# Second attention of a two-layer language model: softmax by TensorE in PSUM after the turn, instead of ScalarE and VectorE before it

## The chip, the cores and the metric

The kernel runs on one NeuronCore of a Trainium2 chip. The metric is the device time of the whole program in microseconds. Before the change it is 5177.2 us, the median of 3 runs (5175.48 to 5177.86).

## What is computed

Two batches of 1024 tokens of width 1024 pass through a token map and two layers; each layer is an attention and a mixture of low-rank experts, each behind a layer norm and added to its input. The change lies in the second attention. It has 32 query heads and 8 key and value heads of 32 columns, and it keeps, in each query's row, only the 128 largest scores:

```python
draft = jnp.einsum('bhqd,bhkd->bhqk', qr, kr)
draft = draft + jnp.where(causal_future, neg, jnp.asarray(0.0, dtype))
_, draft_indices = jax.lax.top_k(draft, num_remain)
mask = jnp.full((B, H, Sq, Sq), neg, dtype)
mask = mask.at[b_idx, h_idx, s_idx, draft_indices].set(0.0)
mask = jnp.where(causal_future[None, None, :, :], neg, mask)
scores = jnp.einsum('bhqd,bhkd->bhqk', qr, kr) / np.sqrt(HD).astype(np.float32) + mask
attn = jax.nn.softmax(scores, axis=-1)
out = jnp.einsum('bhqk,bhkd->bhqd', attn, v)
```

Here `num_remain` is 128 and the rows have up to 1024 keys.

## The kernel before

The program is a sequence of blocks: token map, projection, first attention, mixture, projection, second attention (`kept_attention`, L807), last mixture. Each block writes its engines' instruction streams by hand, and semaphores order them; nothing is scheduled by a compiler.

`kept_attention` works on 32 pairs of heads (m = 0, 1). The queries of a head are 8 tiles i of 128 rows. Tile i has (i + 1) x 128 keys, so a pair's lower triangle is 2 x 36 blocks of 128 x 128, SEG = 4608 columns a head. The work is a pipeline over slots s (L870): in slot s

- the scores of pair s + 1 are computed by TensorE (`scores`, L926) and fetched from PSUM by VectorE with the row's maximum (`fetch`, L1262);
- pair s is searched: in five passes p ScalarE counts how many scores of a row lie under a threshold (`count`, L1014, a Sign with a running sum, L1030), VectorE counts the two narrowest tiles itself (`count_short`, L1087), and `narrow` (L1134) makes the next threshold from the counts. L1127 (`start`) and L1166 (the end of `narrow`) increment the semaphore `t_ready` that ScalarE waits for, and ScalarE's `signs_done` is what `narrow` waits for ahead of L1140;
- pair s - 1 is chosen and kept: `rank_some` (L1180) and `choose` (L1188) find the limit exactly, and `keep` (L1252) multiplies the exponentials by (score >= limit), with the row sum (L1257);
- pair s - 2 goes to the values stage: TensorE turns the blocks (`turn`, L942), ScalarE copies them to `probT` (`evac`, L993), TensorE multiplies by V (`values`, L958), and VectorE normalises (`normalise`, L1270).

The exponentials of pair s are made by ScalarE behind its counts of passes 2, 3 and 4 (`exps`, L1036), with the negated maximum as bias. The row sums are inverted in pass 4 (`invert`, L1278), spread over 512 columns, turned by TensorE (`turn_inverse`, L950) and copied to `invT` (L999). Scores x have two buffers, the exponentials two more in `arena`, `ps_t` has three banks and `ps_o` one.

Which part of VectorE's work comes in which pass is written out by hand (`part`, L1311): the ranks in passes 0 and 1, `choose` at the end of 1; keeps of 7, 5 and 2 tiles in passes 2, 3, 4; fetches of 4, 8 and 4 tiles there; `normalise` at the end of pass 2. ScalarE's 24 evacuations stand between and behind its counts of passes 0 and 1 (`evacs`, L1010), the last four of each pass behind all its counts. TensorE's stream in a slot is the inverse's turn, then for every two chunks two turns and the value products of the two chunks before, and at last the 16 score tiles, two of which fit ahead of VectorE's fetches. SP's queue loads queries and keys a group (two pairs) ahead, stores the outputs of a slot, and loads the next values when they are stored (L894).

Slots run from -1 to 33. Those from 4 to 29 are a hardware loop whose body is two slots (L878).

The values stage in TensorE's stream:

```python
if n >= 2:
    pe.wait_ge(probT_ready, (s - 2) * TURNED + (n - 1))
for c in range(0, w, P):
    at = ps_seg(m, i) + a + c
    mm = nc.tensor.transpose(ps_t[:, (n + 1) % 3, c:c + P], prob[:, par, at:at + P], ident[:, :])
mm.then_inc(turn_done, 1)
```

## Time and profile before

| what | value |
|---|---|
| median of 3 runs | 5177.2 us |
| profiled execution: its own time | 5178.5 us |
| profiled execution: span, first to last instruction | 5176.7 us |
| PE busy, share of the span | 3755.9 us, 73% |
| VectorE (DVE) busy | 3509.0 us, 68% |
| ScalarE (ACT) busy | 3166.3 us, 61% |
| mean granted TensorE clock | 0.831 of full speed |

The page also draws the span in 40 slices of about 129 us. The second attention takes slices 18 to 37, from about 2250 to 4855 us: there VectorE shows 8 tenths and ScalarE 9 in nearly every slice, PE about 5, with a granted clock of 6 to 7 tenths.

A line of a group reads: line, engine, operation, output <- inputs by the program's names, their shapes, count, then busy us and mean ns of one, then the engine's idle time just before these instructions and what ended it. "issue" is time in which the engine waited for nothing that the profile shows. Busy time alone does not tell what sets the end of a stage; the order in time and the waits do.

### The profile page before, as it was taken

The page shows a single profiled execution, that of the slowest core. Times are in us where ns is not written, and L with a number is a line of the kernel's source. Part 1 is how long each engine was busy: PE and PEld are TensorE (multiplying, and loading weights), DVE is VectorE, ACT ScalarE, POOL GpSimd, SP SyncE. Part 2 cuts the span into 40 slices and gives each one's busy share as a digit, 9 for nine tenths or more (in the row PEclk, how much of TensorE's full clock was granted, in tenths as well). Part 3 has the DMA queues.
Part 4 walks back from the last instruction along what each step waited for, and adds up shares of the span by engine and source line. Part 5 has one row for each costly group of instructions (what it writes and reads, how often), then busy time and mean ns, then how long its engine had stood idle before and what let it go on. Part 6 is the DMA issues. An engine that isn't in the chain of part 4 may idle for free. (4 is left out here: it accounts for less than half of the span.)

```text
span 5176.7 us, 79684 instructions
## 1 busy us (share of the span) xinstructions
PE 3755.9 (73%) x23338; PEld 2210.1 (43%) x23480; DVE 3509.0 (68%) x10383; ACT 3166.3 (61%) x7058; POOL 288.7 (6%) x213
## 2 busy tenths in 40 slices
PE   6998999998999999934555355555555555554699
PEld 2444766666444444412333233333333333332454
DVE  3654777776333356548888888888888888887444
ACT  1123777776000011259999599999999999999200
POOL 2332000000000023300000000000000000000000
PEclk9999999999999999966766566767766667766899
DMA  3325223232211112310111011110011110110222
GB/s 139 74 64 162 71 61 79 53 78 82 68 49 49 44 46 69 85 41 1 26 27 26 1 26 26 25 25 12 18 26 26 23 26 4 26 26 6 78 86 77
DMA packets 276875, 249.81 MB, mean 48 GB/s; under 512 B 170048, under 2 KB 209232, under 8 KB 276432
## 3 DMA queue, kind: packets, MB, share of 16 engines
q1 hardware_dynamic: 275888, 245.13, 18.0%
q14 instruction: 324, 2.65, 0.2%
q8 instruction: 119, 1.95, 0.2%
q0 software_dynamic: 544, 0.07, 0.0%
HBM read 167.56 MB, written 77.59 MB: 47 GB/s over the span
## 5 line engine op out<-in xcount | busy, mean ns | idle before, releaser
L1030 ACT ACTIVATE a_sign<-a_x,a_state 128x384 fp8e4<-128x384 f32 (+5 forms) x1536 | 1343.0, 876 | 126.3 <-DVE a_state L1166 87.9
L936 PE MATMUL a_ps_s<-k,q 128*128 128x512 bf16 (+3 forms) x1474 | 500.7, 486 | 692.0 <-DVE a_x L1267 661.7
L947 PE MATMUL a_ps_t<-ident,arena 128*128 128x128 f32 x2304 | 484.6, 355 | 194.3 <-ACT a_invT L999 130.6
L936 PEld LDWEIGHTS a_ps_s<-k,q 128*128 128x128 bf16 x1536 | 168.6, 131 | 916.3 <-DVE a_x L1267 749.8
L965 PE MATMUL a_ps_o<-a_probT,vals 128*32 128x128 f32 x4608 | 404.9, 325 | 185.1 <-ACT a_probT L995 184.7
L947 PEld LDWEIGHTS a_ps_t<-ident,arena 128*128 128x128 f32 x2304 | 338.6, 180 | 333.4 <-ACT a_invT L999 143.4
L721 ACT ACTIVATE a_prob<-a_x_neg,a_shift 128x640 f32<-128x640 f32 (+7 forms) x512 | 397.1, 776 | 80.4 <-DVE a_x_neg L764 61.9
L1267 DVE TENSOR_SCALAR_CACHE_REDUCE a_x<-a_ps_s 128x128 f32<-128x128 f32 (+7 forms) x512 | 383.7, 754 | 85.2 <-PE a_ps_s L939 59.9
L995 ACT COPY a_probT<-a_ps_t 128x512 f32<-128x512 f32 (+3 forms) x768 | 345.9, 475 | 111.1 <-PE a_ps_t L947 110.5
L764 DVE TENSOR_SCALAR_CACHE_REDUCE a_x_neg<-a_ps_s 128x640 f32<-128x640 f32 (+7 forms) x512 | 378.7, 751 | 38.8 <-PE a_ps_s L645 25.6
L1177 DVE MAX8 a_nine<-a_below 128x8 f32<-128x256 f32 (+6 forms) x448 | 371.0, 828 | 32.9
L965 PEld LDWEIGHTS a_ps_o<-a_probT,vals 128*32 128x32 f32 x4608 | 266.6, 128 | 293.9 <-ACT a_probT L995 267.9
L660 PE MATMUL a_ps_t<-ident,a_prob 128*128 128x128 f32 x2304 | 363.7, 281 | 33.4 <-ACT a_prob L721 19.6
L1257 DVE SCALAR_TENSOR_TENSOR arena<-a_x,a_limit,arena 128x1024 f32<-128x1024 f32 (+6 forms) x449 | 379.2, 878 | 5.1 <-issue 4.5
L1174 DVE SCALAR_TENSOR_TENSOR a_below<-a_last,a_x 128x256 f32<-128x256 fp8e4 (+6 forms) x448 | 362.3, 809 | 7.5 <-ACT a_last L1030 7.4
L642 PE MATMUL a_ps_s<-k,q 128*128 128x512 bf16 (+3 forms) x1456 | 320.1, 326 | 26.8 <-DVE a_x_neg L764 12.3
L347 PE MATMUL p_ps_qkv<-wqkv,p_hT 128*128 128x512 f32 x768 | 337.8, 597 | 1.7 <-ACT p_hT L385 1.2
L347 PE MATMUL p_ps_qkv<-arena,p_hT 128*128 128x512 f32 x768 | 337.8, 597 | 1.6 <-ACT p_hT L385 1.2
L1030 ACT ACTIVATE a_last<-a_x,a_state 128x384 fp8e4<-128x384 f32 (+5 forms) x384 | 333.1, 868 | 5.2
L774 DVE COPY a_probT<-a_ps_t 128x384 f32<-128x384 f32 (+3 forms) x384 | 221.6, 577 | 166.8 <-PE a_ps_t L660 165.3
L1042 ACT ACTIVATE arena<-a_x,a_shift 128x256 f32<-128x256 f32 (+6 forms) x448 | 334.0, 813 | 0.0
L385 ACT COPY p_hT<-p_ps_h 128x512 f32<-128x512 f32 x64 | 34.4, 589 | 440.9 <-PE p_ps_h L334 440.9
(216 smaller groups left out, 5947.7 us busy)
## 6 DMA issues: line engine op xcount, KB each, us to landing
q<-qk SPq DMA_DIRECT2D x256, 256.0 KB, 4.9
qk<-p_qkT SPq DMA_DIRECT2D x32, 960.0 KB, 6.2
h_rows<-h SPq DMA_DIRECT2D x32, 512.0 KB, 6.8
k<-qk SPq DMA_DIRECT2D x256, 64.0 KB, 5.2
m_o<-o SPq DMA_DIRECT2D x32, 512.0 KB, 5.5
m_h<-h SPq DMA_DIRECT2D x32, 512.0 KB, 5.3
h<-tok_h SPq DMA_DIRECT2D x16, 512.0 KB, 4.0
arena<-in_wo SPq DMA_DIRECT2D x16, 512.0 KB, 11.3
```

The lines of the kernel that those rows point to most:

```text
L347: m = nc.tensor.matmul(ps_qkv[:, n * BANK:(n + 1) * BANK], hT[:, par, k * P:(k + 1) * P], w[:, k, n * BANK:(n + 1) * BANK], start=(k == 0) ...
L660: mm = nc.tensor.transpose(ps_t[:, n % 2, c * P:(c + 1) * P], prob[:, s % 2, (a + c) * P:(a + c + 1) * P], ident[:, :])
L721: nc.scalar.activation(prob[:, s % 2, 0:w], x_neg[:, s % 4, 0:w], ACT.Exp, scale=-1.0, bias=shift[:, s % 4:s % 4 + 1], accum_out=total[:, ...
L764: nc.vector.tensor_scalar(x_neg[:, c, 0:w], ps_s[:, s % 2, 0:w], -1.0, None, ALU.mult, ALU.min, accum_out=shift[:, c:c + 1]).then_inc(shif ...
L936: nc.tensor.matmul(ps_s[:, n % 2, a:a + w], q[:, y, head, i * P:(i + 1) * P], k[:, y, a:a + w], start=(y == 0), stop=False, skip_group_che ...
L947: mm = nc.tensor.transpose(ps_t[:, (n + 1) % 3, c:c + P], prob[:, par, at:at + P], ident[:, :])
L965: mm = nc.tensor.matmul(ps_o[strip:strip + DH, c:c + P], v[:, at * DH:(at + 1) * DH], probT[:, (n + m) % 4, b * P:(b + 1) * P], start=(at ...
L1030: ins = nc.scalar.activation(to, x[:, par, at:at + w], ACT.Sign, scale=-1.0, saturate=False, bias=state[:, par, 0, n:n + 1], accum_out=sta ...
L1174: lambda: nc.vector.scalar_tensor_tensor(out=below[:, r, 0:w], in0=last[:, at:at + w], scalar=2 * WIDE if n in SHORT else WIDE, in1=x[:, y ...
L1177: lambda: nc.vector.max(nine[:, n, 1:9], below[:, r, 0:w]),
L1257: return nc.vector.scalar_tensor_tensor(out=prob[:, y, at:at + w], in0=x[:, y, at:at + w], scalar=limit[:, r:r + 1], in1=prob[:, y, at:at ...
L1267: nc.vector.tensor_scalar(x[:, y, at:at + w], ps_s[:, n % 2, 0:w], 1.0, None, ALU.mult, ALU.max, accum_out=top[:, y, n:n + 1]).then_inc(x_ ...
```

## The change

- `keep` becomes `mark` (VectorE): it writes a bf16 mask, 0 or -1e18, from the scores and the limit, with no multiplication and no row sum.
- The exponentials of x on ScalarE in passes 2 to 4 are removed. TensorE turns the scores themselves, and adds to the turned block in PSUM the negated maximum of each query (as three bf16 parts that add up to it, turned once a slot, and spread over the keys by a matmul with a matrix of ones in three rows) and the turned mask (70 matmuls of 128 columns a slot; the first tile of a head has none). ScalarE's evacuation is the exponential.
- V has 32 columns of ones beside its 32 columns, so each head's products have their row sums in 32 rows of PSUM below the outputs. `ps_o` has two banks for that, `ps_t` two instead of three.
- `normalise` takes the reciprocal of all of `ps_o`, 128 x 1024, and multiplies each head's 32 rows by the sums' inverses. `invert`, `turn_inverse` and the copy to `invT` are gone; the maximum's turn and its copy of 48 rows stand in their place.
- Scores have three buffers, two of them in `arena`, since a score lives until its turn. So the slots repeat only after 6, and the loop's body is six slots: 4 to 27 are in the loop.
- VectorE waits in pass 2 for the last turn ahead of its marks, since there is one mask buffer; it no longer waits for the exponentials. PE's turn waits one evacuation sooner than before, having a bank less.

```diff
         c_at, t_at = g * P + (2 * y + m) * DH, b * T
-        sp.dma_start(o_dram[ds(c_at, DH), ds(t_at, T)].rearrange("d (h c) -> h d c", h=2),
-                     o[2 * m * DH:(2 * m + 2) * DH, :]).then_inc(done, 16)
+        sp.dma_start(o_dram[ds(c_at, DH), ds(t_at, T)], o[2 * m * DH:(2 * m + 1) * DH, :]).then_inc(done, 16)
...
         probT = sb("probT", [P, 4, BANK])
-        o = sb("o", [P, BANK])
+        o, inv = sb("o", [P, T]), sb("inv", [P, T])
         sign, last = sb("sign", [P, SEG + P], FP8), sb("last", [P, 2 * SEG], FP8)
         below = sb("below", [P, 2, T])
-        top, shift = sb("top", [P, 2, 2 * TT]), sb("shift", [P, 2, 2 * TT])
-        total, inv = sb("total", [P, 2, 2 * TT]), sb("inv", [P, 2 * TT])
-        inv_wide, invT = sb("inv_wide", [P, BANK]), sb("invT", [P, BANK])
+        top, rest = sb("top", [P, 2 * TT]), sb("rest", [P, 2 * TT])
+        top_b = sb("top_b", [P, 2, 2 * TT], BF16)
+        top_parts, topT = sb("top_parts", [P, 3, P]), sb("topT", [SPLITS * 2 * TT, P], BF16)
+        row_of, rows = sb("row_of", [SPLITS * 2 * TT, 2 * TT, P], BF16), sb("rows", [SPLITS * 2 * TT, 2 * TT])
...
+        ps_s, ps_t, ps_o = ps("ps_s", [P, 2, 2 * BANK]), ps("ps_t", [P, 2, BANK]), ps("ps_o", [P, 2 * BANK])
...
         def over_slots(eng, slot):
 
             for s in range(-1, FIRST_LOOP):
-                slot(s, s % 2, stages(s))
+                slot(s, s % BODY, stages(s))
             with eng.Fori(0, LOOPS) as r:
-                for c in (0, 1):
-                    slot(r * 2 + (FIRST_LOOP + c), c, ALL)
-            for s in range(FIRST_LOOP + 2 * LOOPS, PAIRS + 2):
-                slot(s, s % 2, stages(s))
+                for c in range(FIRST_LOOP, FIRST_LOOP + BODY):
+                    slot(r * BODY + c, c % BODY, ALL)
+            for s in range(FIRST_LOOP + BODY * LOOPS, PAIRS + 2):
+                slot(s, s % BODY, stages(s))
...
                     def turn(n, m, i, a, w):
-                        if n >= 2:
-                            pe.wait_ge(probT_ready, (s - 2) * TURNED + (n - 1))
+
+                        to = ps_t[:, (n + 1) % 2, 0:w]
+                        pe.wait_ge(probT_ready, (s - 2) * TURNED + max(n, 1))
                         for c in range(0, w, P):
                             at = ps_seg(m, i) + a + c
-                            mm = nc.tensor.transpose(ps_t[:, (n + 1) % 3, c:c + P], prob[:, par, at:at + P], ident[:, :])
+                            nc.tensor.matmul(to[:, c:c + P], xs[old][:, at:at + P], ident[:, :], start=(c == 0), stop=False,
+                                             is_transpose=True, skip_group_check=True)
+                        mm = nc.tensor.matmul(to.rearrange("p (b c) -> p b c", c=P), row_of[:, m * TT + i, :],
+                                              topT[:, :].unsqueeze(1).to_broadcast([SPLITS * 2 * TT, w // P, P]),
+                                              start=False, stop=(i == 0), skip_group_check=True)
+                        for c in range(0, w if i else 0, P):
+                            at = ps_seg(m, i) + a + c
+                            mm = nc.tensor.matmul(to[:, c:c + P], mask[:, at:at + P], ident_b[:, :], start=False,
+                                                  stop=True, skip_group_check=True)
                         mm.then_inc(turn_done, 1)
 
-                    def turn_inverse():
-                        pe.wait_ge(inv_ready, s - 1)
+                    def turn_top():
+                        pe.wait_ge(top_ready, s - 1)
                         if not (isinstance(s, int) and s == 2):
                             pe.wait_ge(probT_ready, (s - 2) * TURNED)
-                        for c in range(0, BANK, P):
-                            mm = nc.tensor.transpose(ps_t[:, 0, c:c + P], inv_wide[:, c:c + P], ident[:, :])
-                        mm.then_inc(turn_done, 1)
+                        nc.tensor.transpose(ps_t[:, 0, 0:P], top_parts[:, old, :], ident[:, :]).then_inc(turn_done, 1)
...
+                                half, at = 2 * m * DH, a // P + b
+                                mm = nc.tensor.matmul(ps_o[half:half + 2 * DH, i * P:(i + 1) * P], v[:, at, :],
                                                       probT[:, (n + m) % 4, b * P:(b + 1) * P], start=(at == 0),
-                                                      stop=(at == i), tile_position=(0, strip))
+                                                      stop=(at == i), tile_position=(0, half))
...
+                        pe.wait_ge(mask_ready, (s - 2) * NS + NS)
                         if not (isinstance(s, int) and s == 2):
                             pe.wait_ge(o_ready, s - 2)
-                        turn_inverse()
+                        turn_top()
...
+
                     def evac(n, m, i, a, w):
                         act.wait_ge(turn_done, (s - 2) * TURNED + (n + 2))
-                        nc.scalar.copy(probT[:, n % 4, 0:w], ps_t[:, (n + 1) % 3, 0:w]).then_inc(probT_ready, 1)
-
-                    def inverse_evac():
+                        nc.scalar.activation(probT[:, n % 4, 0:w], ps_t[:, (n + 1) % 2, 0:w], ACT.Exp).then_inc(probT_ready, 1)
+
+                    def top_evac():
                         act.wait_ge(turn_done, (s - 2) * TURNED + 1)
-                        nc.scalar.copy(invT[:, :], ps_t[:, 0, :]).then_inc(probT_ready, 1)
+                        nc.scalar.copy(topT[:, :], ps_t[0:SPLITS * 2 * TT, 0, 0:P]).then_inc(probT_ready, 1)
...
-                    def exps(n, y):
-
-                        m, i = TILES[n]
-                        at, w = ps_seg(m, i), (i + 1) * P
-                        if i:
-                            ins = nc.scalar.activation(prob[:, y, at:at + w], x[:, y, at:at + w], ACT.Exp,
-                                                       bias=shift[:, y, n:n + 1])
-                        else:
-                            ins = nc.scalar.activation(prob[:, y, at:at + w], x[:, y, at:at + w], ACT.Exp,
-                                                       bias=shift[:, y, n:n + 1], accum_out=total[:, y, n:n + 1])
-                        ins.then_inc(exp_done, 1)
-
-
-                    EXPS = {2: range(0, 6), 3: range(6, 11), 4: range(11, 2 * TT)}
                     for p in range(PASSES):
                         if st["search"]:
                             count(p)
                         else:
                             for n in range(NS):
                                 evacs(p * NS + n)
-                        if st["search"] and p in EXPS:
-                            if p == 2 and st["value"]:
-                                act.wait_ge(turn_done, (s - 2) * TURNED + TURNED)
-                            for n in EXPS[p]:
-                                exps(n, par)
 
...
                 nc.vector.memset(two[:, :], 2.0)
+                nc.vector.memset(top_parts[:, :, :], 0.0)
+                nc.vector.memset(v[:, :, DH:2 * DH], 1.0)
+                of = [ident[0:SPLITS * 2 * TT, c * 2 * TT:(c + 1) * 2 * TT] for c in range(SPLITS)]
+                nc.vector.tensor_tensor(rows[:, :], of[0], of[1], ALU.add)
+                dve.drain()
+                nc.vector.tensor_tensor(rows[:, :], rows[:, :], of[2], ALU.add)
+                dve.drain()
+                nc.vector.tensor_copy(row_of[:, :, :], rows[:, :].unsqueeze(2).to_broadcast([SPLITS * 2 * TT, 2 * TT, P]))
                 quantile, per_sign, aim = (table[:, k_, :] for k_ in range(3))
...
-                        nc.vector.tensor_scalar(shift[:, z, :], top[:, z, :], -1.0, None, ALU.mult)
+                        hi, mid, lo = (top_parts[:, (turn_of + 1) % 3, c * 2 * TT:(c + 1) * 2 * TT] for c in range(SPLITS))
+                        nc.vector.tensor_scalar(top_b[:, 0, :], top[:, :], -1.0, None, ALU.mult)
                         dve.drain()
                         nc.vector.tensor_scalar(var_h[:, :], var[:, :], -0.5, None, ALU.mult)
-                        dve.drain()
+                        nc.vector.scalar_tensor_tensor(out=rest[:, :], in0=top[:, :], scalar=-1.0, in1=top_b[:, 0, :],
+                                                       op0=ALU.mult, op1=ALU.subtract)
+                        nc.vector.tensor_copy(hi, top_b[:, 0, :])
+                        dve.drain()
+                        nc.vector.tensor_copy(top_b[:, 1, :], rest[:, :])
+                        dve.drain()
+                        nc.vector.tensor_copy(mid, top_b[:, 1, :])
+                        nc.vector.tensor_tensor(lo, rest[:, :], top_b[:, 1, :], ALU.subtract).then_inc(top_ready, 1)
...
-                    def keep(r):
...
+                    def mark(r):
 
                         m, i = RANKED[r]
-                        n = TILES.index((m, i))
                         at, w = ps_seg(m, i), (i + 1) * P
-                        return nc.vector.scalar_tensor_tensor(out=prob[:, y, at:at + w], in0=x[:, y, at:at + w],
-                                                              scalar=limit[:, r:r + 1], in1=prob[:, y, at:at + w],
-                                                              op0=ALU.is_ge, op1=ALU.mult,
-                                                              accum_out=total[:, y, n:n + 1])
+                        return nc.vector.tensor_scalar(mask[:, at:at + w], old_x[:, at:at + w], limit[:, r:r + 1], MASKED,
+                                                       ALU.is_lt, ALU.mult)
...
-                        nc.vector.tensor_scalar(x[:, y, at:at + w], ps_s[:, n % 2, 0:w], 1.0, None, ALU.mult, ALU.max,
-                                                accum_out=top[:, y, n:n + 1]).then_inc(x_ready, 1)
+                        nc.vector.tensor_scalar(new_x[:, at:at + w], ps_s[:, n % 2, 0:w], 1.0, None, ALU.mult, ALU.max,
+                                                accum_out=top[:, n:n + 1]).then_inc(x_ready, 1)
 
                     def normalise():
 
                         dve.wait_ge(pv_done, (s - 2) * (NC // 2) + NC // 2)
-                        dve.wait_ge(probT_ready, (s - 2) * TURNED + 1)
                         if not (isinstance(s, int) and s == 2):
                             dve.wait_ge(o_out, (s - 2) * 32)
-                        nc.vector.tensor_tensor(o[:, :], ps_o[:, :], invT[:, :], ALU.mult).then_inc(o_ready, 1)
-
-                    def invert():
-
-                        dve.drain()
-                        nc.vector.reciprocal(inv[:, :], total[:, y, :])
-                        dve.drain()
-                        nc.vector.tensor_copy(inv_wide[:, :].rearrange("p (j q c) -> p j q c", j=4, q=4),
-                                              inv[:, :].rearrange("p (q j) -> p j q", j=4).unsqueeze(3).to_broadcast(
-                                                  [P, 4, 4, DH])).then_inc(inv_ready, 1)
+                        nc.vector.reciprocal(inv[:, :], ps_o[:, :])
+                        dve.drain()
+                        for m in range(2):
+                            half = 2 * m * DH
+                            ins = nc.vector.tensor_tensor(o[half:half + DH, :], ps_o[half:half + DH, :],
+                                                          inv[half + DH:half + 2 * DH, :], ALU.mult)
+                        ins.then_inc(o_ready, 1)
 
...
-                                dve.wait_ge(exp_done, (s - 1) * (2 * TT) + 2 * TT)
+                        if p == 2 and st["value"]:
+                            dve.wait_ge(turn_done, (s - 2) * TURNED + TURNED)
...
-                                keep(r).then_inc(prob_ready, 1)
+                                mark(r).then_inc(mask_ready, 1)
...
-                        if p == 4 and st["keep"]:
-                            invert()
+                        if p == 4:
+                            dve.drain()
                         if p == 4 and st["score"]:
-                            dve.drain()
...
-        vals1 = sb(ctx, "vals1", [P, TT * DH])
+        vals1 = sb(ctx, "vals1", [P, TT, 2 * DH])
```

## Rows read from the trace of the kernel before

**Rows 1.** Windows: length, busy us (xcount) of PE, PEld, DVE, ACT, POOL, granted clock.

```profile
2390.00:4835.00 2445.00, 1340.05 (x8630) 821.51 (x8687) 2072.01 (x6573) 2222.78 (x4935) 0.00 (x0) 0.69 0.09 21
```

**Rows 2.** VectorE's timeline, one slot: start us, us, engine, line, operation, [idle before].

```profile
4171.10 0.17 DVE L1127 SCALAR_TENSOR_TENSOR a_state<-a_mean,a_tmp 128x14 f32<-128x14 f32 x1
...
4250.13 0.17 DVE L1127 SCALAR_TENSOR_TENSOR a_state<-a_mean,a_tmp 128x14 f32<-128x14 f32 x1
...
4265.78 0.18 DVE L1166 COPY_PREDICATED a_state<-a_open,a_new 128x14 f32<-128x14 int32 x1
...
4282.90 0.17 DVE L1140 TENSOR_TENSOR a_state<-a_state,search 128x14 f32<-128x14 f32 x1 [1.67 <-ACT a_sign L1030]
...
4284.81 0.18 DVE L1166 COPY_PREDICATED a_state<-a_open,a_new 128x14 f32<-128x14 int32 x1
...
4299.13 0.18 DVE L1166 COPY_PREDICATED a_state<-a_open,a_new 128x14 f32<-128x14 int32 x1
...
4313.19 0.18 DVE L1166 COPY_PREDICATED a_state<-a_open,a_new 128x14 f32<-128x14 int32 x1
...
4327.50 0.17 DVE L1127 SCALAR_TENSOR_TENSOR a_state<-a_mean,a_tmp 128x14 f32<-128x14 f32 x1
...
4330.90 0.48 DVE L1095 SCALAR_TENSOR_TENSOR a_sign<-a_x,a_state,a_two 128x256 fp8e4<-128x256 f32 x1 [2.81 <-issue]
```

**Rows 3.** Groups by line, the second attention, ScalarE.

```profile
L1042 ACT ACTIVATE arena<-a_x,a_shift 128x896 f32<-128x896 f32 x415 | 310.0, 814 | 0.0
...
L995 ACT COPY a_probT<-a_ps_t 128x128 f32<-128x128 f32 (+1 forms) x744 | 335.2, 475 | 108.2 <-PE a_ps_t L947 107.6
```

**Rows 4.** Groups by shape, before 2500 us, ScalarE.

```profile
L237 ACT ACTIVATE tok_h<-tok_ps_h 128x1024 f32<-128x1024 f32 x16 | 16.0, 1025 | 18.5 <-PE tok_ps_h L223 15.8 <-DMA h<-tok_h 2.7
```

**Rows 5.** Groups by shape, the second attention, VectorE.

```profile
L1257 DVE SCALAR_TENSOR_TENSOR arena<-a_x,a_limit,arena 128x1024 f32<-128x1024 f32 x62 | 79.0, 1275 | 0.1
...
L1257 DVE SCALAR_TENSOR_TENSOR arena<-a_x,a_limit,arena 128x256 f32<-128x256 f32 x60 | 28.9, 482 | 4.8 <-issue 4.5
...
L1276 DVE TENSOR_TENSOR a_o<-a_ps_o,a_invT 128x512 f32<-128x512 f32 x31 | 21.3, 686 | 22.4 <-PE a_ps_o L965 21.9 <-issue 0.5
...
L1159 DVE RECIPROCAL a_rs<-a_span 128x14 f32<-128x14 f32 x88 | 21.2, 241 | 6.4
...
L1100 DVE TENSOR_SCALAR a_last<-a_x,a_state 128x256 fp8e4<-128x256 f32 x60 | 18.5, 350 | 4.3
...
L1281 DVE RECIPROCAL a_inv<-a_total 128x16 f32<-128x16 f32 x31 | 7.8, 253 | 7.1 <-issue 5.7
```

**Rows 6.** Groups by shape, before 2400 us, VectorE.

```profile
L106 DVE TENSOR_SCALAR arena<-h_rows,p_mv,p_rstd 128x1024 f32<-128x1024 f32 x32 | 26.0, 813 | 2.5
...
L1638 DVE TENSOR_TENSOR m_y<-m_ps_y,m_h 128x1024 f32<-128x1024 f32 x16 | 19.6, 1225 | 155.9 <-PE m_ps_y L1501 155.9
...
L779 DVE RECIPROCAL a_inv<-a_total 128x8 f32<-128x8 f32 x64 | 12.3, 192 | 0.0
```

**Rows 7.** TensorE's timeline, two slots: turns, bias and score matmuls, values.

```profile
3563.38 1.97 PE L947 MATMUL a_ps_t<-ident,arena 128*128 128x128 f32 x8
...
3583.05 0.22 PE L939 MATMUL a_ps_s<-a_bias_b,a_ident_b 128*128 128x128 bf16 x1
...
3583.11 0.38 PE L936 MATMUL a_ps_s<-k,q 128*128 128x256 bf16 x2
...
3608.15 0.97 PE L936 MATMUL a_ps_s<-k,q 128*128 128x512 bf16 x4
...
3608.95 0.22 PE L939 MATMUL a_ps_s<-a_bias_b,a_ident_b 128*128 128x128 bf16 x1
...
4851.34 1.09 PE L947 MATMUL a_ps_t<-ident,arena 128*128 128x128 f32 x8
...
4852.36 1.94 PE L965 MATMUL a_ps_o<-a_probT,vals 128*32 128x128 f32 x32
```

**Rows 8.** VectorE's timeline, last normalisation of the second attention.

```profile
4854.35 0.69 DVE L1276 TENSOR_TENSOR a_o<-a_ps_o,a_invT 128x512 f32<-128x512 f32 x1 [21.89 <-PE a_ps_o L965]
```

66 lines of the change are left out of this document (33 added, 33 removed).

## The prediction

> **What bounds the kernel now.** I read the busy time by stage first. Over the 2445 us of the second attention VectorE is busy 2072 us and ScalarE 2223 us [rows 1]. ScalarE has the larger sum, so it looks like the bound, but both are close together, and neither sum tells who waits for whom. So next comes VectorE's timeline, at the instructions that hand a new threshold to ScalarE (L1127 once a slot, L1166 four times) [rows 2]. From one to the next the passes last 15.65, 19.03, 14.32, 14.06 and 14.31 us: a slot of 77.4 us. The slot before took 79.0 (4171.10 to 4250.13), the mean is 78.2. In this slot VectorE waits for ScalarE's counts only in pass 1, 1.67 us ahead of L1140. Otherwise it goes from one of its own instructions to the next. So VectorE sets passes 0, 2, 3 and 4, and ScalarE, with the values stage of TensorE that it evacuates, sets the end of pass 1. Without that wait passes 0 and 1 would take 34.7 - 1.7 = 33.0 us. In every second slot VectorE also stands 2.81 us for nothing that the profile shows, at the first instruction behind the loop's return [rows 2].
>
> This decides what the parts are worth: what leaves ScalarE in passes 2 to 4 is nearly free of profit, what VectorE gains or loses there counts in full.
>
> **ScalarE.** The exponentials of x go, 16 a slot at 814 ns, some 13 us [rows 3]. All lie in passes 2 to 4, beside VectorE. The only part on the path is the tail by which pass 0's counts start late, about 1 us. The 24 evacuations become exponentials. From PSUM with no bias the nearest row is the tanh, 1025 ns for 1024 columns [rows 4], against 475 ns for 384 on average of the copies [rows 3]: 0.86 ns a column between them, the columns' own rate, so I take no extra (at most 24 x 0.1 us).
>
> **VectorE, marks.** 14 keeps, from 482 ns at 256 columns to 1275 at 1024 [rows 5], so 880 at the mean of 640, become one-source mask writes with no sum. The nearest rows of that kind are 350 ns at 256 columns [rows 5] and 813 at 1024 [rows 6], so 0.6 ns a column instead of 1.03, and 565 to 580 on average. That saves 0.3 us each, 4.2 us a slot: 2.1 in pass 2 (7 marks), 1.1 in pass 3 (5 mostly narrow), 0.95 in pass 4 (2 wide). If the bf16 result forces one column at a time, it is 350 + 768 x 1.03 = 1140 at 1024, and the saving only 1.6 us a slot.
>
> **VectorE, normalise.** Today it is one multiply of 512 columns, 686 ns [rows 5]. It becomes a reciprocal of 1024 columns out of PSUM, then two multiplies of 1024 columns, one behind the other, at 1225 ns each [rows 6] less overlap, 2.4 us together. The reciprocal is the term that matters. The trace has it at 8 columns, 192 ns [rows 6], at 14, 241 ns, and at 16, 253 ns [rows 5]. A copy or an add doesn't get dearer by 61 ns over 8 columns; a reciprocal does: (253 - 192) / 8 = 7.6 ns a column. 1024 columns then take 0.13 + 1024 x 7.6 ns = **7.9 us**. Bounds: from 14 to 16 columns 6 ns, 6.3 us; from 8 to 14 columns 8.2 ns, 8.5 us. The least that I admit is a plain one-column rate, 1.2 us, a rival below. The sum is 7.9 + 0.1 + 2.4 - 0.7 = +9.7 us, all of it in pass 2 between the fetches and the narrowing, where nobody else does VectorE's work. Queued behind it are L1140 and so ScalarE's next counts.
> The Trainium skill ("VectorE: DVE Perf Modes", First, the fixed hardware budget) says that the reciprocal is an iterative divide with a repeat count of 8; with that page's 0.96 GHz I estimate 8.3 ns a column, 8.5 us, and the total would be some 20 us above mine. It speaks against this change, and the rows above agree.
>
> **VectorE, the rest.** invert() goes: its reciprocal of 253 ns, a copy of 512 columns and two drains, 0.8 us in pass 4. The bf16 splits of the maximum add five operations of 14 to 16 columns, 0.17 us each as L1140 in rows 2, with two drains between them: 0.85 us. They cancel.
> New waits: in pass 2 the marks wait for the last turn. By rows 2 pass 2 begins when that stage has just ended, and VectorE gets there over 2 us later, so it costs nothing; it is charged below if the stage grows. PE's first turn waits for the evacuated maximum, ScalarE's first work in a slot, as the inverse does today. SP's queue has the same steps: the stores stand 27 us ahead of what needs them, and the values' load with 128-byte rows has that cover too.
>
> **TensorE.** Three of the four turns of the inverse go, one is left for the maximum. Added per slot: 70 mask matmuls of 128 columns in bf16, the same as the causal bias, which is followed after 0.06 us at the full clock [rows 7], 4.2 us; and 24 row matmuls, 9216 columns in all, by the score matmuls, four of 512 in 0.80 us [rows 7], 3.6 us. So +7.8 us at 2.4 GHz on 18.0 (72 turns at 0.128, 144 value matmuls at 0.061, [rows 7]), and about twice both at 1.2 GHz, where eight turns last 1.97 us instead of 1.09. The granted clock averages 0.69 [rows 1], since PE idles between evacuations; more work in the stage gives fewer idle gaps. 26 to 30 us of work fit into 34.7 us by length, but PE has two score banks, not three, and ScalarE takes the four last chunks of a pass in one go. I take 36 us for passes 0 and 1, between 33.0 (PE and ScalarE fully hidden) and 34.7 + 7.8 = 42.5 (all added work on the path).
>
> **The sum.** Pass 2: 14.3 - 2.1 + 9.7 = 21.9. Pass 3: 14.1 - 1.1 = 13.0, and 13.1 with ScalarE's counts so close under it. Pass 4: 14.3 - 0.95 + 0.05 = 13.4. With 36.0 that is 84.4, and 0.4 for the loop's return, one slot in six: 84.8 us, **+6.6 a slot**, for 30 slots +198. Slot 32 has no counting: -4.2 + 9.7 - 0.8 = +4.7. In slot 33 the values stage stands alone, VectorE waits 21.89 us for it [rows 8]: +7.8 + 9.7 - 0.7 = +16.8. Set-up and first slots: about -0.5. In all +219 us. The profiled execution took 5178.5 us (span 5176.7), 1.3 above the median of the runs, so I forecast 5396 against the median of 5177.2.
>
> **Rivals.** (a) *The reciprocal streams.* The slope of three tiny shapes might not hold over 1024 columns: then it takes 1.2 us, 6.7 less in 32 slots, 5182, and with passes 0 and 1 at their lower end of 33.0 another 90 less, 5092, faster. The point from which it decides is 7.9 - 219 / 32 = 1.1 us for the reciprocal, about 1 ns a column. Against it: three rows on one line of 6 to 8 ns a column. 0.07, of which 0.05 faster.
> (b) *TensorE becomes the bound of passes 0 and 1.* With them at 42.5 us it is 6.5 x 30 = 195 more, 5591. For it: pass 1 already ends on ScalarE and PE, a bank less, and value matmuls with 64 columns of weights instead of 32. If the two halves no longer run side by side, the stage is 9 us longer still. Against it: one slot in two ends by VectorE alone, and idle PE time is there to fill. 0.13. The Trainium skill ("TensorEngine Tiling (Array Packing)", When to Use Tiling) gives 64-column weights two tiles where 32-column ones have four; since the two heads alternate between halves before and after, my sum needs only two.
> (c) *The marks run at one column a cycle.* 2.6 us less saved in 31 slots, +80, 5476. Against it: the fp8 write of 256 columns takes 350 ns where the form with two sources takes 482. 0.1.
> (d) *ScalarE was the bound after all*, and 13 us of exponentials leave the path: then passes 2 to 4 would fall by more than VectorE allows; rows 2 exclude that, and it would come out as (a) at best.
> My forecast has 0.7.
>
> **Numbers.** Own range: reciprocal 6.3 to 8.5 (-51, +20), passes 0 and 1 a few us either way. Down to 5310 and up to 5510 it takes in (c) and half of (b). A measurement of this kernel can tell 0.2%, 10 us, from no change. Faster 0.05 and same 0.02 come from (a); slower 0.93 is the rest.
>
> **What would show it.** The reciprocal's row at 1024 columns, 6.3 to 8.5 us, 32 times; pass 2 at 22 us, passes 3 and 4 at 13 to 13.5; ScalarE busy well under 80% with idle time ended by L1166; mark rows near 570 ns; the mask matmuls 0.06 us apart. Wrong, if the reciprocal's row is under 2 us, or if the time between L1127 and the second L1166 leaves 33 to 40 us.

## The result and the profile after

The changed kernel takes 5380.95 us (median of 4 runs, 5373.36 to 5382.62), the kernel before 5176.34 on the same chip (4 runs). The ratio is 1.0392, interval 1.0374 to 1.041: **slower by 205 us**, where 219 had been forecast. The profiled execution took 5373.36 us (span 5371.5).

First the page of the changed kernel, busy time by engine and the groups that the change touches:

```profile
PE 4044.9 (75%) x26250; PEld 2322.1 (43%) x26392; DVE 3622.6 (67%) x10099; ACT 2837.9 (53%) x6482; POOL 289.1 (5%) x213
...
L1008 ACT ACTIVATE a_probT<-a_ps_t 128x512 f32<-128x512 f32 (+3 forms) x768 | 365.4, 483 | 289.1 <-PE a_ps_t L959 262.2
...
L954 PE MATMUL a_ps_t<-a_topT,a_row_of 48*128 48x512 bf16 (+3 forms) x768 | 289.1, 376 | 0.0
...
L959 PE MATMUL a_ps_t<-a_ident_b,a_mask 128*128 128x128 bf16 x2240 | 275.7, 242 | 0.0
```

ScalarE's evacuations now hold the exponential and last 483 ns on average, where the copies of [rows 3] lasted 475. What is new stands behind the bar: ScalarE waits 262 us for the mask matmul that ends a chunk (108 for the turn in [rows 3]). In the values stage it's TensorE that comes late, more than twice as much as before.

Next VectorE's groups by shape over the second attention:

```profile
L1283 DVE RECIPROCAL a_inv<-a_ps_o 128x1024 f32<-128x1024 f32 x32 | 209.7, 6554 | 39.9 <-PE a_ps_o L976 39.4 <-issue 0.5
...
L1287 DVE TENSOR_TENSOR a_o<-a_ps_o,a_inv 32x1024 f32<-32x1024 f32 x64 | 77.9, 1217 | 2.8
...
L1267 DVE TENSOR_SCALAR a_mask<-arena,a_limit 128x1024 bf16<-128x1024 f32 x45 | 33.4, 741 | 0.1
...
L1267 DVE TENSOR_SCALAR a_mask<-arena,a_limit 128x640 bf16<-128x640 f32 x44 | 23.8, 542 | 0.0
...
L1151 DVE TENSOR_TENSOR a_state<-a_state,search 128x14 f32<-128x14 f32 x128 | 22.3, 174 | 211.9 <-ACT a_sign L1043 206.7 <-issue 4.1
...
L1267 DVE TENSOR_SCALAR a_mask<-arena,a_limit 128x256 bf16<-128x256 f32 x44 | 15.5, 351 | 11.1 <-PE a_ps_t L959 8.0 <-issue 2.7
```

One reciprocal of 6.55 us a slot is the largest group: 210 us, more than the whole difference. The row of L1151 is the instruction that waits for ScalarE's counts; it now waits 207 us in all for ScalarE, against 81 before (L1140). Slot by slot in the timeline, the wait at the end of pass 1 is over 1.7 us in each of slots 4 to 28, and at the end of pass 0 some 3.2 us in 22 of these 25. Before, both stood at 0.7 and 1.7 us, and in one slot of two alone: not in those in which VectorE stands 2.8 us at the loop's return, since it is late itself there.

VectorE's timeline shows pass 2 of one slot, from one handed threshold (L1177) to the next (columns as in [rows 2]):

```profile
3486.52 0.17 DVE L1151 TENSOR_TENSOR a_state<-a_state,search 128x14 f32<-128x14 f32 x1 [1.78 <-ACT a_sign L1043]
...
3488.42 0.18 DVE L1177 COPY_PREDICATED a_state<-a_open,a_new 128x14 f32<-128x14 int32 x1
...
3491.08 3.33 DVE L1267 TENSOR_SCALAR a_mask<-arena,a_limit 128x256 bf16<-128x256 f32 x7 [0.16 <-issue]
...
3496.80 6.55 DVE L1283 RECIPROCAL a_inv<-a_ps_o 128x1024 f32<-128x1024 f32 x1
3503.43 2.45 DVE L1287 TENSOR_TENSOR a_o<-a_ps_o,a_inv 32x1024 f32<-32x1024 f32 x2
3506.05 0.17 DVE L1151 TENSOR_TENSOR a_state<-a_state,search 128x14 f32<-128x14 f32 x1 [0.17 <-issue]
...
3507.95 0.18 DVE L1177 COPY_PREDICATED a_state<-a_open,a_new 128x14 f32<-128x14 int32 x1
```

L1151 at 3506.05 waits for nobody: VectorE sets the end of this pass, and 9.0 of its 19.5 us are the normalisation. The windows of the five passes of this slot and of the whole stage, columns as in [rows 1]:

```profile
3451.00:3469.20 18.20, 16.84 (x108) 9.74 (x108) 14.02 (x40) 14.73 (x35) 0.00 (x0) 0.69 0.00 1
3469.20:3488.50 19.30, 17.30 (x162) 10.95 (x161) 15.51 (x49) 15.45 (x36) 0.00 (x0) 1.00 0.01 1
3488.50:3508.00 19.50, 7.41 (x66) 4.51 (x65) 17.65 (x40) 11.68 (x26) 0.00 (x0) 0.70 0.01 2
3508.00:3521.00 13.00, 8.18 (x32) 3.54 (x32) 11.16 (x41) 10.60 (x24) 0.00 (x0) 0.66 0.00 1
3521.00:3533.90 12.90, 3.11 (x10) 1.28 (x11) 11.77 (x41) 10.60 (x24) 0.00 (x0) 0.74 0.41 95
2387.80:4950.00 2562.20, 1579.49 (x11128) 904.59 (x11186) 2130.70 (x6178) 1889.07 (x4343) 0.00 (x0) 0.74 0.09 19
```

In passes 0 and 1 TensorE is busy 34.1 of 37.5 us (the first busy time behind the length; the second is its weight loads), VectorE 29.5, ScalarE 30.2. Over the stage ScalarE fell to 74% of the time, from 91% in [rows 1], and that bought next to nothing.

Taken from such timelines, the passes have these lengths in us, as means over slots 2 to 30 without slot 8, whose exact selection lasts some 56 us in both kernels. All later pass lengths are made in this way. The forecast's 84.8 holds 0.4 for the loop's return.

| | pass 0 | 1 | 2 | 3 | 4 | 0 + 1 | slot |
|---|---|---|---|---|---|---|---|
| before | 16.8 | 18.3 | 14.5 | 14.0 | 14.5 | 35.1 | 78.1 |
| after | 18.1 | 19.7 | 20.0 | 13.0 | 13.0 | 37.8 | 83.8 |
| forecast | | | 21.9 | 13.1 | 13.4 | 36.0 | 84.8 |

### The profile page after: what moved, and what is told of

It is laid out like the page before. It is cut to its first block and busy times, and to the rows that moved or that the text cites. A ratio compares the mean times of both kernels' runs of the same rounds, so it can differ in the third digit from the quotient of the medians.

```text
span 5371.5 us, 84339 instructions
## 1 busy us (share of the span) xinstructions
PE 4044.9 (75%) x26250; PEld 2322.1 (43%) x26392; DVE 3622.6 (67%) x10099; ACT 2837.9 (53%) x6482; POOL 289.1 (5%) x213
## 3 DMA queue, kind: packets, MB, share of 16 engines
q1 hardware_dynamic: 289072, 245.14, 17.5%
## 5 line engine op out<-in xcount | busy, mean ns | idle before, releaser
L1043 ACT ACTIVATE a_sign<-arena,a_state 128x384 fp8e4<-128x384 f32 (+5 forms) x1056 | 917.6, 871 | 206.3 <-DVE a_state L1177 167.2
L1008 ACT ACTIVATE a_probT<-a_ps_t 128x512 f32<-128x512 f32 (+3 forms) x768 | 365.4, 483 | 289.1 <-PE a_ps_t L959 262.2
L1043 ACT ACTIVATE a_sign<-a_third,a_state 128x384 fp8e4<-128x384 f32 (+2 forms) x480 | 417.3, 871 | 139.2 <-DVE a_state L1177 136.3
L952 PE MATMUL a_ps_t<-ident,arena 128*128 128x128 f32 x1584 | 335.5, 328 | 201.6 <-ACT a_topT L1012 154.7
L976 PE MATMUL a_ps_o<-a_probT,vals 128*64 128x128 f32 x4608 | 362.4, 299 | 0.0
L1275 DVE TENSOR_SCALAR_CACHE_REDUCE arena<-a_ps_s 128x128 f32<-128x128 f32 (+3 forms) x352 | 262.9, 755 | 46.1 <-PE a_ps_s L943 21.6
L659 PEld LDWEIGHTS a_ps_t<-ident,a_prob 128*128 128x128 f32 x2304 | 247.9, 141 | 101.7 <-issue 36.1
L954 PE MATMUL a_ps_t<-a_topT,a_row_of 48*128 48x512 bf16 (+3 forms) x768 | 289.1, 376 | 0.0
L976 PEld LDWEIGHTS a_ps_o<-a_probT,vals 128*64 128x64 f32 x4608 | 265.7, 147 | 42.8 <-issue 15.9
L959 PE MATMUL a_ps_t<-a_ident_b,a_mask 128*128 128x128 bf16 x2240 | 275.7, 242 | 0.0
```

The lines of the kernel that those rows point to most:

```text
L659: mm = nc.tensor.transpose(ps_t[:, n % 2, c * P:(c + 1) * P], prob[:, s % 2, (a + c) * P:(a + c + 1) * P], ident[:, :])
L952: nc.tensor.matmul(to[:, c:c + P], xs[old][:, at:at + P], ident[:, :], start=(c == 0), stop=False, is_transpose=True, skip_group_check=True)
L954: mm = nc.tensor.matmul(to.rearrange("p (b c) -> p b c", c=P), row_of[:, m * TT + i, :], topT[:, :].unsqueeze(1).to_broadcast([SPLITS * 2 ...
L976: mm = nc.tensor.matmul(ps_o[half:half + 2 * DH, i * P:(i + 1) * P], v[:, at, :], probT[:, (n + m) % 4, b * P:(b + 1) * P], start=(at == 0 ...
L1008: nc.scalar.activation(probT[:, n % 4, 0:w], ps_t[:, (n + 1) % 2, 0:w], ACT.Exp).then_inc(probT_ready, 1)
L1043: ins = nc.scalar.activation(to, xs[mine][:, at:at + w], ACT.Sign, scale=-1.0, saturate=False, bias=state[:, par, 0, n:n + 1], accum_out=s ...
```

## The experiments

Ratios are to the kernel before, run on the same chips: 5172.44 us beside the first experiments, 5173.18 beside the next, 5174.61 beside the last three. The theory after the first profile: the reciprocal costs what the kernel lost, and the matmuls added to the values stage cost a second, smaller part that the lighter marks pay for.

### The reciprocal cut to 16 columns

```diff
-                        nc.vector.reciprocal(inv[:, :], ps_o[:, :])
+                        nc.vector.reciprocal(inv[:, 0:16], ps_o[:, 0:16])
```

> The changed kernel with the reciprocal cut to 16 of its 1024 columns (the other columns are multiplied by 1, so all but the first 16 queries of each head are not normalised). All else stays. Theory A, the forecast's: the reciprocal, 6554 ns in the profile of the changed kernel, stands alone on the path of pass 2. Pass 2 falls from 19.6 us by 6.3 to 13.3, just above the 12.8 us that ScalarE's counts and the narrowing need, and the kernel by 6.3 x 32 = 200 us, to about 5180. Theory B, TensorE's longer values stage is what costs and the reciprocal only fills time that VectorE would wait anyway: less than 60 us, so above 5320.

Measured: 5207.92 us, ratio 1.0065 (1.0049 to 1.0082), so 173 us of the 205 go with it (on another chip; by the ratios it's 169). Each of 32 reciprocals became 6.30 us shorter (6554 - 253 ns), 202 us in all, so some 29 us didn't come back. The pass lengths tell where they went: pass 2 is 14.6 us instead of the 13.7 (20.0 - 6.3) that VectorE's own work would need. VectorE's timeline of the pass and ScalarE's beside it:

```profile
3748.86 0.18 DVE L1178 COPY_PREDICATED a_state<-a_open,a_new 128x14 f32<-128x14 int32 x1
...
3761.49 0.17 DVE L1152 TENSOR_TENSOR a_state<-a_state,search 128x14 f32<-128x14 f32 x1 [1.49 <-ACT a_sign L1043]
```

```profile
3749.23 0.60 ACT L1008 ACTIVATE a_probT<-a_ps_t 128x512 f32<-128x512 f32 x1 [1.34 <-PE a_ps_t L959]
3750.32 0.60 ACT L1008 ACTIVATE a_probT<-a_ps_t 128x512 f32<-128x512 f32 x1 [0.49 <-PE a_ps_t L959]
3750.81 0.61 ACT L1043 ACTIVATE a_sign<-arena,a_state 128x384 fp8e4<-128x384 f32 x1
```

The threshold is ready at 3748.86, but ScalarE's queue still holds the last two evacuations, for which it waits on TensorE. Its counts begin 1.95 us late, and VectorE waits 1.49 us for them at the end. VectorE waits there for the counts in nearly every slot, and the pass ends at 14.5 to 14.6 us in nearly all. **There is a second floor under pass 2, 14.5 us, set by the tail of the values stage.** In the changed kernel it lies hidden under the reciprocal. That the tail sets it is read from the timeline; no run shortens the tail alone.

### The reciprocal added to the kernel before

```diff
                         nc.vector.tensor_tensor(o[:, :], ps_o[:, :], invT[:, :], ALU.mult).then_inc(o_ready, 1)
+                        nc.vector.reciprocal(below[:, 1, :], below[:, 0, :])
```

> The kernel before with one reciprocal of 1024 columns, from SBUF to SBUF, ahead of its normalising multiply, whose result nobody uses; in that kernel the two buffers are free there. Theory A: it takes 6.5 us as in the changed kernel and pass 2 of the kernel before is VectorE's, so each of 32 slots is 6.5 us longer: 208 us, about 5385. Theory B: ScalarE's exponentials in passes 2 to 4 leave room, and less than 60 us show. If a reciprocal from SBUF is quicker than one from PSUM, its row tells.

Measured: 5374.73 us, ratio 1.039 (1.0373 to 1.0407), +202 us, and its group reads:

```profile
L1276 DVE RECIPROCAL a_below<-a_below 128x1024 f32<-128x1024 f32 x32 | 209.6, 6548 | 21.9 <-PE a_ps_o L965 21.4 <-issue 0.5
```

Pass 2 goes from 14.5 to 20.7 us; the others stay within 0.2. One instruction a slot, with nothing else of the change, makes the kernel before as slow as the changed one. It reads SBUF, the changed kernel PSUM, and both take 6.55 us.

### What a reciprocal costs by size

```diff
+                nc.vector.memset(third[:, :], 1.5)
+                dve.drain()
+                for size in (8, 16, 32, 64, 128, 256, 512, 1024):
+                    nc.vector.reciprocal(inv[:, 0:size], third[:, 0:size])
+                    dve.drain()
```

> The changed kernel with eight more reciprocals ahead of its first slot, SBUF to SBUF, every input 1.5, of 8, 16, 32, 64, 128, 256, 512 and 1024 columns. The forecast's line, 0.13 us and 7.6 ns a column, gives 7.9 us at 1024, the changed kernel shows 6554 ns from PSUM. Theory D: the rate is 6.2 to 6.4 ns a column at every width, as from 14 to 16 columns, and the row of 8 columns has a smaller fixed part: about 0.33 us at 32, 1.7 at 256, 3.3 at 512, 6.5 at 1024. Theory E: small shapes cost 7.6 ns a column, and the rate falls with the width: 0.37 us at 32, and the slope between 32 and 64 is still over 7 ns. If the rate hangs on the values or on PSUM, 1024 columns of 1.5 from SBUF differ from 6554 ns.

One run, with these lines added to the set-up of the changed kernel. The groups by shape:

```profile
L1073 DVE RECIPROCAL a_inv<-a_third 128x1024 f32<-128x1024 f32 x1 | 6.6, 6554 | 0.1
...
L1073 DVE RECIPROCAL a_inv<-a_third 128x128 f32<-128x128 f32 x1 | 1.0, 953 | 0.1
...
L1073 DVE RECIPROCAL a_inv<-a_third 128x32 f32<-128x32 f32 x1 | 0.4, 354 | 0.1
...
L1073 DVE RECIPROCAL a_inv<-a_third 128x8 f32<-128x8 f32 x1 | 0.2, 203 | 0.1
```

From 8 to 1024 columns the cost is 0.153 us and 6.25 ns a column: (6554 - 203) / 1016. It is the column count that costs, neither the values nor where they lie. This run took 5404.15 us, and nothing is concluded from its time. The 8-column row of [rows 6] shows 192 ns, where this line gives 203. Those 11 ns, spread over 8 columns, made my slope 7.6.
The Trainium skill ("VectorE: DVE Perf Modes", First, the fixed hardware budget) has an iterative divide with a repeat count of 8; with the page's 0.96 GHz I had estimated 8.3 ns a column. The runs show 6.25, which by that clock I estimate at 6 cycles a column. That a reciprocal costs far more than one cycle a column, the run confirms; that the repeat count is the number of cycles, it does not.

### The changed kernel without the row and mask matmuls

```diff
                                 mm = nc.tensor.matmul(to[:, c:c + P], xs[old][:, at:at + P], ident[:, :], start=(c == 0),
-                                             stop=False, is_transpose=True, skip_group_check=True)
-                        mm = nc.tensor.matmul(to.rearrange("p (b c) -> p b c", c=P), row_of[:, m * TT + i, :], ...)
-                        for c in range(0, w if i else 0, P):
-                            mm = nc.tensor.matmul(to[:, c:c + P], mask[:, at:at + P], ident_b[:, :], ...)
+                                             stop=(c + P == w), is_transpose=True, skip_group_check=True)
```

> The changed kernel without the 24 row matmuls and 70 mask matmuls of a slot: TensorE turns the scores and ScalarE takes their exponential with no maximum taken off and nothing masked. Theory A: passes 0 and 1 are held by the length of TensorE's work, busy 34.1 of 37.5 us; without some 8 us of it they fall to what VectorE alone needs, 33.0 to 34.5 us, 3 to 4.5 us in 31 slots, so 95 to 140 us less, 5240 to 5285. Theory C, the stage is held by the alternation of TensorE and ScalarE over two banks and not by the length of the work: passes 0 and 1 stay above 36.5 us and the kernel falls by less than 35 us.

Measured: 5241.75 us, ratio 1.0138 (1.0121 to 1.0155), 139 us less than the changed kernel. Passes 0 and 1 are 34.1 us together instead of 37.8, the others keep their lengths within 0.2. That makes 3.7 us a slot, 110 in 30 slots, in the stretch where I had charged 0.9 over before. VectorE's waits for the counts fall back to what they are in the kernel before (0.6 and 1.0 us on average in passes 0 and 1, against 0.5 and 1.0). So the lost bank and the 64 columns of weights, which this run keeps, don't lengthen these passes. The rest of the 139 lies behind the last counting slot, where the stage stands alone. The windows of slot 33's values stage, of the changed kernel and of the kernel before:

```profile
5005.00:5045.20 40.20, 38.99 (x311) 24.31 (x311) 0.77 (x2) 12.04 (x25) 0.00 (x0) 0.79 0.26 102
5005.00:5022.00 17.00, 15.83 (x76) 8.81 (x76) 0.77 (x2) 3.76 (x9) 0.00 (x0) 0.50 0.62 240
```

```profile
4832.40:4854.30 21.90, 21.33 (x220) 16.48 (x220) 0.06 (x1) 11.01 (x25) 0.00 (x0) 0.89 0.37 147
4832.40:4837.50 5.10, 4.54 (x22) 3.25 (x24) 0.06 (x1) 2.13 (x6) 0.00 (x0) 0.52 1.01 395
```

Here TensorE is busy 39.0 of 40.2 us, and VectorE waits 39.44 us for it, against 21.89 in [rows 8]. Without the added matmuls VectorE's group in that stretch reads:

```profile
L1276 DVE RECIPROCAL a_inv<-a_ps_o 128x1024 f32<-128x1024 f32 x1 | 6.6, 6558 | 22.2 <-PE a_ps_o L969 22.2
```

So they cost 17.2 us where nothing covers them, not 7.8. TensorE's timeline of that stage shows one reason, in a chunk that starts at the low level (1.2 GHz) and two later ones at the high level (2.4 GHz):

```profile
5021.71 0.60 PE L954 MATMUL a_ps_t<-a_topT,a_row_of 48*128 48x512 bf16 x1
5022.25 0.40 PE L959 MATMUL a_ps_t<-a_ident_b,a_mask 128*128 128x128 bf16 x4
...
5024.95 0.23 PE L954 MATMUL a_ps_t<-a_topT,a_row_of 48*128 48x128 bf16 x1
5025.11 0.23 PE L959 MATMUL a_ps_t<-a_ident_b,a_mask 128*128 128x128 bf16 x1
...
5032.49 0.39 PE L954 MATMUL a_ps_t<-a_topT,a_row_of 48*128 48x512 bf16 x1
5032.81 0.40 PE L959 MATMUL a_ps_t<-a_ident_b,a_mask 128*128 128x128 bf16 x4
5033.05 0.61 PE L952 MATMUL a_ps_t<-ident,arena 128*128 128x128 f32 x4
```

The four masks take 0.24 us to the next turn (32.81 to 33.05), the 0.06 each that I had. The row matmul of 512 columns takes 0.32 us before the masks start, not the 0.20 of a score matmul, and 0.54 at the low level (21.71 to 22.25). One of 128 columns takes 0.16 (24.95 to 25.11). So its columns go at 0.42 ns each ((0.32 - 0.16) / 384), close to the score matmuls' 0.39 (0.20 / 512), and each row matmul costs a fixed 0.11 us besides; why, no run shows. At 2.4 GHz alone the added work is 70 x 0.06 + 9216 x 0.42 ns + 24 x 0.11 = 10.7 us.

The other reason is the clock. The second rows of the two windows show that the stage runs at the low level for its first 17 us, against 5 before. TensorE stood idle ahead of it in both kernels, 14 us and 17 us. If I halve these stretches, the stages would last some 31.7 and 19.4 us at the high level: about 12 of the 17 us are work, an estimate, and some 5 are the longer low stretch. What makes that stretch longer isn't shown.

### The kernel before with two banks for the turned blocks

```diff
-        ps_s, ps_t, ps_o = ps("ps_s", [P, 2, 2 * BANK]), ps("ps_t", [P, 3, BANK]), ps("ps_o", [P, BANK])
+        ps_s, ps_t, ps_o = ps("ps_s", [P, 2, 2 * BANK]), ps("ps_t", [P, 2, BANK]), ps("ps_o", [P, BANK])
```

(Each turn also waits for one evacuation more. The bank taken is one of `ps_t`; the prediction's "two score banks, not three" means these, the score banks are two in both kernels.)

> The kernel before with two banks for the turned blocks instead of three, and each turn waiting for one evacuation more. Theory A: the bank is worth little, since the evacuation of a bank ends while the other is turned; passes 0 and 1 stay within 0.3 us of their 34.8, and the kernel within 10 us of 5176. Theory C, the lost bank stops TensorE: passes 0 and 1 get 1.5 to 3 us longer, 45 to 90 us in all.

Measured: 5163.3 us over 10 runs, ratio 0.998 (0.9971 to 0.999): a bank less costs nothing, and is even 9 us faster. Pass 1 is 17.9 us instead of 18.3. Why isn't settled. It takes the bank out of the list of what made passes 0 and 1 longer.

### Evacuations ahead of the next threshold

In ScalarE's timeline of the changed kernel, between pass 4 and pass 0, the engine stands idle, since its first evacuations are queued behind the wait for the new slot's threshold (L1138), on which they don't depend:

```profile
3448.78 0.18 ACT L1043 ACTIVATION_READ_ACCUMULATOR a_last<-arena,a_state 128x1 f32 x1
3451.34 0.26 ACT L1012 CAST a_topT<-a_ps_t 48x128 bf16<-48x128 f32 x1 [2.38 <-DVE a_state L1138]
3452.38 0.28 ACT L1008 ACTIVATE a_probT<-a_ps_t 128x128 f32<-128x128 f32 x1 [0.78 <-PE a_ps_t L954]
```

```diff
+                        if p == 0 and st["value"]:
+                            top_evac()
+                            for c in CH[:EARLY]:
+                                evac(*c)
```

(ahead of the wait, with EARLY = 2.)

> The changed kernel with ScalarE's copy of the turned maximum and its first two evacuations moved ahead of the wait for the next slot's first threshold, where ScalarE stands idle 2.4 us at the end of pass 4. Theory A: passes 0 and 1 are held by the length of TensorE's stage, which begins with that copy, so the stage begins and ends 2 to 2.5 us earlier: passes 0 and 1 35.2 to 35.8 us, 30 slots, 60 to 75 us less, about 5312. Theory C: the evacuations' places among ScalarE's counts hold the stage; then TensorE waits at the next one and the kernel falls by less than 20 us.

Measured: 5307.2 us, ratio 1.0256 (1.0239 to 1.0273), 74 less. Pass 0 falls from 18.1 to 15.9 us, and passes 0 and 1 together are 2.5 us shorter. TensorE's wait for the evacuated maximum falls from 204 us over the slots to 137, 2.2 us a slot: the stage begins that much earlier, and the passes end that much earlier. With the run without the added matmuls, where a shorter stage ended them earlier, this shows that the values stage sets their end, by its start and by its length. The waits of both kernels, the changed one first (us in total, times, longest):

```profile
PE a_ps_t L952 <- ACT a_topT L1012: 204.3, 29, 8.3
```

```profile
PE a_ps_t L952 <- ACT a_topT L1012: 137.0, 30, 8.3
```

### The reciprocal between two block-transposes

The row sums stand in 32 equal partitions beside each head's values, so 31 of 32 reciprocals are repeats. Transposed in 32x32 blocks, one column in 32 holds them all:

```diff
-                        nc.vector.reciprocal(inv[:, :], ps_o[:, :])
+                        nc.vector.transpose(wide[:, :], ps_o[:, :])
+                        dve.drain()
+                        nc.vector.reciprocal(narrow_inv[:, :], wide[:, :].rearrange("p (b c) -> p b c", c=32)[:, :, 0])
+                        dve.drain()
+                        nc.vector.transpose(inv[:, :], narrow_inv[:, :].unsqueeze(2).to_broadcast([P, 32, 32]))
```

> The changed kernel with the reciprocal of 1024 columns replaced: VectorE turns the 32 x 32 blocks of the values' bank into SBUF (the sums stand in 32 equal rows, so they are then in 32 equal columns), inverts one column of each block, 32 in all, and turns them back from a broadcast. Two turns at the column rate are 1.1 to 1.2 us each, the reciprocal about 0.35, two more drains: 2.8 us in place of 6.55. Pass 2 falls from 20.0 on average by 3.7 to 16.3, which is still over the 14.5 at which the run with 16 columns stopped; 3.7 x 32 = 118 us, about 5263. If the block turn costs more than a column a cycle from PSUM or from a broadcast, say 2 us each, the gain is 2 us a slot, 64 in all.

```profile
L1284 DVE STREAM_TRANSPOSE a_wide<-a_ps_o 128x1024 f32<-128x1024 f32 x32 | 39.9, 1246 | 40.4 <-PE a_ps_o L977 39.9 <-issue 0.5
L1288 DVE STREAM_TRANSPOSE a_inv<-a_narrow_inv 128x1024 f32<-128x1024 f32 x32 | 39.9, 1246 | 2.4
L1286 DVE RECIPROCAL a_narrow_inv<-a_wide 128x32 f32<-128x32 f32 x32 | 11.3, 354 | 2.3
```

Measured: 5263.88 us, ratio 1.0172 (1.0155 to 1.0189), 117 less. 2.85 us of instructions do what 6.55 did, and pass 2 falls from 20.0 to 16.5.

**Both edits together:**

> The two changes of e6_early and e7_two_turns together. They lie in different passes, so Theory A has them add up: 5381 - 70 - 118 = 5193, still 0.4% above the kernel before. If pass 2 is then held by ScalarE's late start into it, which an earlier end of the stage also shortens, it can be 10 to 20 us less.

Measured: 5189.6 us over 10 runs, ratio 1.003 (1.0021 to 1.004). The passes are 15.7, 19.4, 16.5, 13.1 and 13.1. The two gains add up, since they lie in different passes.

### Work moved out of the full pass

Pass 2 is still set by VectorE, while in pass 1 VectorE waits for ScalarE. The test whether any rank failed (transpose, four casts, maximum) needs only what pass 1 has computed:

```diff
                             if p == 1:
                                 choose()
-                            if p == 2:
                                 any_failing()
```

> The kernel with both edits (early evacuations, reciprocal between two block-transposes), and any_failing moved from pass 2 to the end of pass 1, where VectorE waits about 1.9 us for ScalarE's last counts. Theory: any_failing (1.15 to 1.3 us of VectorE work) leaves pass 2, whose end VectorE's chain sets, and goes into idle time: pass 2 from 16.5 to 15.2 us, above the 14.5 us at which ScalarE's late start holds it; 30 slots by 1.2 us make -38, some 5150 us, under the kernel before. Rival: pass 1 becomes longer by as much, since the wait there ends with TensorE's stage: no gain, 5190.

Measured: 5143.02 us (5 runs), ratio 0.9941 (0.9928 to 0.9955): **32 us faster than the kernel before**, and the first version of the changed idea that is. Pass 2 is 14.8 us, and pass 1 is 19.5, 0.1 longer: VectorE's wait at its end falls from 2.1 us to 0.7 on average, so the test went into idle time. VectorE's timeline of pass 2:

```profile
3324.41 0.18 DVE L1182 COPY_PREDICATED a_state<-a_open,a_new 128x14 f32<-128x14 int32 x1
...
3334.32 2.45 DVE L1296 TENSOR_TENSOR a_o<-a_ps_o,a_inv 32x1024 f32<-32x1024 f32 x2
3336.93 0.17 DVE L1156 TENSOR_TENSOR a_state<-a_state,search 128x14 f32<-128x14 f32 x1 [0.17 <-ACT a_sign L1048]
...
3338.84 0.18 DVE L1182 COPY_PREDICATED a_state<-a_open,a_new 128x14 f32<-128x14 int32 x1
```

The pass took 14.43 us, and VectorE waits for ScalarE's counts at its end, if only 0.17 us: in this slot it has reached the floor of the first experiment. The gain of 47 us over the version with both edits is more than the 38 expected, mostly since I had counted the instructions alone (1.2 us): in place, with its drains, the test makes the marks begin 2.7 us after the threshold on average over the slots, without it 1.3. The 1.4 us between them make 42 us.

**Four evacuations early instead of two** (EARLY = 4):

> The same with four evacuations early instead of two. Theory: TensorE's stage sets the end of passes 0 and 1, so that what starts it earlier shortens them by 0.5 to 1 us a slot: -15 to -30, 5125 to 5135 us. Rival: ScalarE starts its counts of that pass later, and VectorE waits for them: no gain or a few us worse than the kernel with two.

Measured: 5158.66 us (8 runs), ratio 0.9968 (0.9957 to 0.9978), 16 us worse than with two. Passes 0 and 1 are 16.1 and 19.6 us, against 15.7 and 19.5. The rival held: what goes ahead of the counts delays them. VectorE waits 0.8 us for the counts at the end of pass 0 instead of 0.35, and TensorE's wait for the evacuated maximum stays (125 us against 122), so its stage began no earlier.

**The same move in the kernel before, with two banks for the turned blocks:**

> The kernel before with two score buffers alternating and the same move of any_failing. In half of its slots VectorE is busy through pass 1, so most of the move is a shift from one full pass to another: 0 to -15 us, 5150 to 5163. If it gains 30 or more, the move and not the changed way of attention is what the version above wins by.

Measured: 5169.32 us (11 runs), ratio 0.9993 (0.9984 to 1.0002). Pass 2 falls from 14.6 to 13.2 us, and pass 1 grows from 17.9 to 18.9, pass 0 by 0.3. The move alone gains nothing there. It pays where pass 1 ends on TensorE and ScalarE and VectorE has time to spare. At 13.2 us the pass also lies under the 14.5 at which the changed kernel stops: that floor comes with the changed values stage.

How much of the 32 us the changed attention itself has won is open. The kernel before with two banks is at a ratio of 0.998, which leaves 0.4%, some 20 us. And the changed kernel's loop has a body of six slots instead of two. Before, the 12 slots behind a return last 79.15 us and the others 77.4; in the fastest version 3 slots do, 78.1 against 75.8. From these I estimate 21 us for the returns before and 7 after, so up to 14 us could come from the longer body alone. The kernel before with a body of six slots was not run.

## Why the prediction was right, and where it was off

**The mechanism held.** Taking the exponentials from ScalarE bought next to nothing (read from the pass lengths and waits; no run takes them alone), VectorE's reciprocal fell on the path in full, and passes 3 and 4 shrank to what ScalarE's counts allow. The reciprocal put into the kernel before costs +202 us, and taken out of the changed kernel leaves +36. The forecast of 5396 us was 15 above the measured 5381. That it came so near is in part luck, since several terms were mis-sized, and the errors cancel: 43 us too much for the reciprocal, some 16 for the rest of pass 2 and some 24 for pass 4 and the loop's return stand against 54 too little for passes 0 and 1 and some 14 in slots 32 and 33.

- *"1024 columns then take 0.13 + 1024 x 7.6 ns = 7.9 us".* It is 6.55, so 1.35 us a slot too much, 43 us in 32. The slope came from rows of 8 and 16 columns on different lines, where 11 ns of other causes count as 1.4 ns a column. The bound from below, 6.3 us, had been nearer.
- *"I take 36 us for passes 0 and 1".* It is 37.8, so 1.8 us too little, 54 us in 30 slots. Two sizes were behind it. The row matmul was taken at a score matmul's rate, 0.20 us for 512 columns, and takes 0.32, with a fixed 0.11 us in each of 24. And less of it fills gaps than I had charged: 3.7 us of the added work lengthen the two passes, as the run without it shows. In every second slot VectorE alone had set their end, and I had counted on that cover. But those were the slots in which VectorE stood 2.8 us behind the loop's return, and with a body of six slots the change itself leaves one such in six; now pass 1 ends on ScalarE and TensorE in all.
- *Pass 2, "14.3 - 2.1 + 9.7 = 21.9".* It is 20.0. The reciprocal makes 1.35 us of that. Taken apart from start to start over slots 4 to 28, the seven marks save 2.3 us, not 2.1, and the four fetches behind them take 2.25 us instead of 2.9, which I hadn't foreseen (why isn't shown); against that, pass 2 lasted 14.5 us on average before, not the 14.3 of the one slot.
- *The marks, "565 to 580 on average".* 542 ns at the mean width of 640; 741 at 1024 instead of 813. Rival (c) is out.
- *Pass 4 at 13.4* came out at 13.0, *pass 3 at 13.1* at 13.0. The stop of 2.81 us behind the loop's return [rows 2], for which I had kept 0.4 us a slot, falls into pass 0 of slots 10, 16 and 22. It costs nothing there: it takes the place of the 3.2 us that VectorE waits in the others, and pass 0 lasts 18.2 us with it and without it.
- *Evacuations "no extra".* 483 against 475 ns: right.
- *Slot 33, "+7.8 + 9.7 - 0.7 = +16.8".* The wait for the stage grew by 17.5 us (39.44 - 21.89) and the normalisation by 8.4, together 25.9. The 7.8 was taken at the high level, without the row matmuls' fixed part, and the stage spends 17 us at the low level where it had spent 5.
- *"In pass 2 the marks wait for the last turn ... it costs nothing."* True in the 30 full slots. In slot 32, where no counts hold VectorE back, they wait 8.0 us for TensorE, and that slot grew by some 10 us, not 4.7.
- *First slots, "about -0.5".* From the start of the span to slot 2's first threshold it gained 9.8 us (2387.84 against 2397.66). 4.2 of it is slot 1 (71.0 us instead of 75.1), which has marks and no normalisation; I had forgotten that it gets the saving without the price. The other 5.6 lie ahead of that and may be no effect at all: in the run with 16 columns, with one memset more ahead of this point, it lies at 2398.30, and in the others of the kernel before with edits at 2389.72 to 2394.74.

The spans differ by 194.8 us: -9.8 up to slot 2, +173 for 30 slots at 5.76 (forecast +198), +10 and +25.9 for slots 32 and 33, and about -4 that I can't place.

**Rival (b)**, TensorE the bound of passes 0 and 1, had 0.13 at 42.5 us. Its mechanism is there, as both the run without the adds and the one with early evacuations show, but at 2.7 us above before and not 7.4. **Rival (a)**, a reciprocal that streams, is out by its row. What I had missed altogether is the floor of 14.5 us under pass 2. Without a reciprocal it would hold back some 30 us. (a) would have just cleared it: with a reciprocal of 1.2 us VectorE needs 20.0 - 5.35 = 14.65 us.

## What to carry to other kernels

Before a row sum is put beside the values to save its handling, ask in how many columns its reciprocal is then taken: on VectorE that count is the cost, and two block-transposes around a narrow reciprocal cost less than half of the wide one. Take work off the engine that ends each pass, not off the one that is busiest overall; and when the largest term is gone, look which wait ends the pass next, since engines' queues in fixed order hold floors (here evacuations ahead of counts) that no busy time shows. A price per column should come from rows whose widths differ by much, or from the bound that a wide row gives.

## What the runs showed of the hardware

- A reciprocal on VectorE: 203 ns at 8 columns, 354 at 32, 953 at 128, 6554 at 1024, the same from SBUF and from PSUM. At 1024 columns it is 5.4 times a two-source multiply (1217 ns).
- A block-transpose of 128x1024 takes 1246 ns, both from PSUM and from an operand that repeats each column 32 times.
- A bf16 matmul of 512 moving columns with 48 rows of weights takes 0.32 us at 2.4 GHz from its start to that of the next, where the score matmuls of [rows 7] take 0.20; at 128 columns it takes 0.16. Both fit 0.42 ns a column and a fixed 0.11 us; the 0.54 us at 512 columns and 1.2 GHz fit twice that rate and the same 0.11.
- Alone behind an idle TensorE (14 us), the stage with the added matmuls ran at a granted clock of 0.50 for its first 17 us, and the stage before, behind 17 us of idling, at 0.52 for 5 us.
- The multiply on 32 partitions takes as long as on 128: 1217 ns for 1024 columns, against 1225 in [rows 6].
